# Attention block with layer norm and a quantised layer on one core: TensorE takes the score products two slots at a time, and SyncE issues all the loads of the row layout

## The chip, the cores and the metric

The kernel runs on one core of one Trainium2 chip. The metric is the device time of one execution in microseconds (us). The time of the kernel before is the median of three timed runs. One further execution was taken by the hardware profiler, and all rows below come from that one.

## What is computed

There are 16 batches of 256 tokens with 128 features, and 16 heads of width 8. In every batch the reference does this (cut to what matters):

```python
mod = (silu(c) @ wmod).reshape(16, 6, 1, -1)        # sa, ca, ga, sb, cb, gb; ga and gb kept away from 0
h = layernorm(x) * (1 + ca) + sa
qkv = h @ W_qkv + b_qkv                              # q, k, v: 16 heads of 8
energy = einsum('bqhe,bkhe->bqhk', q, k)
attn = softmax(energy, axis=-1) / sqrt(128)
o = einsum('bihv,bvhd->bihd', attn, v).reshape(16, 256, 128)
x = x + ga * (o @ W_out + b_out)
h = layernorm(x) * (1 + cb) + sb
x = x + gb * (fp6_blocks(h) @ fp6_blocks(weight).T + bias)   # blocks of 32, grid e2m3, one scale per block
```

## The kernel before

All five engines run one software pipeline over batches. The outer loop on each engine is `for b in STEPS`, with b from -4 to 17, and inside it are 16 **slots** s = 0 to 15, one per head of batch b. In slot s of step b TensorE computes two score products, each as two matmuls of 256 columns:

- `scores2(b, s, t)` (line 809) writes the transposed scores of head s of batch b, with the row maxima subtracted, into one of **two** PSUM banks `ps_p2`. ScalarE reads it with `exponentials` (line 551) and writes `probs`. The product of slot s waits for the exponential of slot s - 2.
- `scores1` (line 794) works `LEAD = 20` slots ahead: it writes the plain scores of a later head into one of **three** banks `ps_p1`. VectorE reads it with `maxima` (line 684) for the row maxima. The product of a slot waits for the maxima of the slot three before.

The two products use opposite halves of the 128 array rows (`q_rows` and `k_rows` at partitions 0 to 63 or 64 to 127), so their matmuls are written alternately: one of `scores1`, one of `scores2`, one of `scores1`, one of `scores2`.

Between the slots TensorE does all its **other** products, each behind a slot named in the code. Below they have short names: `tx` (transposes of the normalised x, line 835, slot 0), v3 (`values(b-1, 3)`, slot 1), `hd` (transposes of the quantised rows, line 890, slot 1), `pq` and `pk` (projections to q and k, line 851, slots 2 and 4), `to` (`transpose_o`, line 868, slot 3), `lin` (line 896, slot 3), `tn` (`transpose_norm`, line 876, slot 5), v0 (`values(b, 0)`, line 824, slot 6), `po` (`project_out`, line 882, slot 6), `pv` (`project_v`, line 845, slot 7), `tm` (`transpose_max`, line 858, slots 8 and 14), v1 (slot 10) and v2 (slot 13). `values(b, v)` is 16 matmuls at 32 columns of weights that need the exponentials of slots 4v to 4v + 3.

ScalarE runs its exponentials in the same 16 slots. Behind some it copies PSUM banks out: `save_hT` (line 524, slot 1), `oT`, `hdT` and `onT` (line 555, slots 1, 2, 5), `save_qk` (lines 531 and 532, slots 3 and 5), `save_v` (line 537, slot 7), `save_maxT` (line 543, slots 8 and 14). VectorE runs maxima in the same slots with the layer norms and residuals between them.

q and k are projected for pairs of batches. `tx`, `pq` and `pk` run in odd steps b = 1 to 11 only (in the start also at b = -3 and -2), and `stats1` and `aggregate1` on VectorE (slots 4 and 5) in even steps 0 to 10 only. GpSimd makes the low part of q and k (`low_part`), and SyncE stores high and low parts to `parts_dram` (`store_parts`, lines 358 and 363). Then `lay_out(eng, p, kind, r)` (line 330) reads them back into `q_rows` and `k_rows`, 512 KB for each of kind q, k and half r = 0, 1. Pair p is first read by `scores1` in slot 12 of the next even step. SyncE issues the two with r = 0. ScalarE issues the two with r = 1 in slots 11 and 12 of the odd step, and each waits for the store of its kind. SyncE also carries the row maxima of the next batch into `q_rows` (`place_max`, line 370, half 0 and half 1). `scores2` needs half 0 in slot 0 and half 1 in slot 8 of the next step.

The order on each engine is the order in which the code is written.

## Time and profile of the kernel before

| | |
|---|---|
| median of three timed runs | 344.18 us (343.35 to 344.89) |
| the profiled execution | 341.19 us |
| its span in the trace | 339.3 us |
| granted TensorE clock, mean of the span | 0.923 |
| TensorE, VectorE, ScalarE, GpSimd busy | 82%, 72%, 61%, 51% |
| one odd step (b = 9), sc14 to sc14 | 224.45 - 205.75 = 18.70 us |
| one even step (b = 10), sc14 to sc14 | 240.08 - 224.45 = 15.63 us |

In what follows sc9 means both score products of slot 9, exp9 and max9 the exponential and the maxima of slot 9. The busy time of TensorE counts matmuls of both halves of the array rows, and matmuls are pipelined, so its share alone doesn't say that TensorE is the bound. Which engine sets the pace is read in the timeline of a step: who waits for whom. The profiled execution is 3 us faster than the median of the timed runs.

### The profile page before, as it was taken

How to read it: one execution, taken by the hardware profiler on the slowest of the kernel's cores; microseconds unless marked ns; L12 is line 12 of the kernel's file. 1: busy time of each engine (PE TensorE's matmuls, PEld its weight loads, DVE VectorE, ACT ScalarE, POOL GpSimd, SP SyncE). 2: the span in 40 equal slices, each digit the busy share in tenths (PEclk: the TensorE clock that was granted, in tenths of full speed). 3: DMA queues.
4: the chain of work that ended last, by engine and by line, in shares of the span. 5: the costliest groups of instructions: out<-in, count | busy, mean ns of one | idle time of the engine just before them, and what ended most of it. 6: DMA issues, size and time to landing. Idle time of an engine off the chain costs nothing.

```text
span 339.3 us, 7143 instructions
## 1 busy us (share of the span) xinstructions
PE 279.7 (82%) x2506; PEld 171.2 (50%) x2506; DVE 243.4 (72%) x581; ACT 207.5 (61%) x404; POOL 174.5 (51%) x330
## 2 busy tenths in 40 slices
PE   0831886989999999999998899899989999999742
PEld 0310764545555555555655565556555656555421
DVE  6577775667897679767976797679768878872243
ACT  6262014577668667777677667776777776677510
POOL 5910122316665656566665657575757364645620
PEclk9975555899999999999999999999999999999985
DMA  4679189016911692169316931495149510100000
GB/s 150 199 269 226 35 288 236 9 36 251 251 50 34 265 244 59 35 256 209 103 33 238 214 114 36 192 223 150 36 175 237 152 37 18 35 20 17 2 15 15
DMA packets 23970, 43.81 MB, mean 129 GB/s; under 512 B 2144, under 2 KB 7408, under 8 KB 23936
## 3 DMA queue, kind: packets, MB, share of 16 engines
q1 hardware_dynamic: 20128, 36.03, 35.0%
q10 hardware_dynamic: 3808, 7.34, 9.0%
q8 instruction: 20, 0.33, 0.4%
q14 instruction: 14, 0.11, 0.1%
HBM read 23.93 MB, written 18.91 MB: 126 GB/s over the span
## 4 chain that ended last, share of the span: by engine, by line
PE 55%; ACT 12%; issue 10%; DVE 9%; DMA 9%; POOL 4%; SPq 1%; ACTq 0%; DVEq 0%; POOLq 0%
PE ps_o L824 16%; PE ps_p L794 15%; PE ps_p L809 7%; ACT probs L551 5%; PE ps_pre L851 4%; DVE neg_max L684 3%; DMA parts_dram<-qk_parts 3%; PE ps_post L882 3%; PE ps_pre L845 3%; DMA k_rows<-parts_dram 3%; ACT qk_full_sb L531 2%; ACT qk_parts L532 2%; DMA q_rows<-maxT 2%; PE ps_post L890 2%; PE ps_pre L858 2%
## 5 line engine op out<-in xcount | busy, mean ns | idle before, releaser
L684 DVE TENSOR_REDUCE neg_max<-ps_p 128x2 f32<-128x512 f32 x256 | 165.4, 683 | 49.0 <-PE ps_p L794 48.0
L551 ACT ACTIVATE probs<-ps_p 128x512 f32<-128x512 f32 x256 | 146.2, 596 | 77.5 <-PE ps_p L809 73.8
L809 PE MATMUL ps_p<-q_rows,k_rows 64*128 64x256 f32 x512 | 117.1, 327 | 13.9 <-ACT probs L551 9.7
L794 PE MATMUL ps_p<-k_rows,q_rows 62*128 62x256 f32 x512 | 119.9, 339 | 8.1 <-DMA k_rows<-parts_dram 8.1
L794 PEld LDWEIGHTS ps_p<-k_rows,q_rows 62*128 62x128 f32 x512 | 79.4, 198 | 48.0 <-DVE neg_max L684 22.5
L809 PEld LDWEIGHTS ps_p<-q_rows,k_rows 64*128 64x128 f32 x512 | 74.3, 189 | 24.6 <-ACT probs L551 18.2
L824 PE MATMUL ps_o<-probs,v_aug 128*32 128x256 f32 x1024 | 69.4, 389 | 0.9 <-ACT probs L551 0.9
L429 POOL CAST max_parts<-neg_max 128x16 fp32r<-128x16 f32 x32 | 6.3, 196 | 74.3 <-DVE neg_max L684 74.3
L824 PEld LDWEIGHTS ps_o<-probs,v_aug 128*32 128x32 f32 x1024 | 26.9, 110 | 21.0 <-ACT probs L551 1.4
L448 POOL TENSOR_TENSOR rstd<-ve,minus_half 128x2 f32<-128x2 f32 x16 | 11.3, 704 | 35.1 <-DVE ve L609 35.1
L319 POOL TENSOR_TENSOR qk_parts<-qk_full_sb,qk_parts 128x512 fp32r<-128x512 f32 x14 | 17.7, 1266 | 17.0 <-ACT qk_parts L532 17.0
L851 PE MATMUL ps_pre<-hT,wqkv_sb 128*128 128x512 f32 x28 | 17.5, 709 | 9.2 <-ACT hT L524 5.8
L704 DVE TENSOR_TENSOR x<-ps_post,x_res 128x256 f32<-128x256 f32 x16 | 6.7, 420 | 15.5 <-PE ps_post L882 15.5
L537 ACT ACTIVATE v_aug<-ps_pre 128x256 f32<-128x256 f32 x16 | 6.1, 383 | 16.2 <-PE ps_pre L845 16.0
L543 ACT ACTIVATE maxT<-ps_pre 16x256 fp32r<-16x256 f32 x32 | 11.4, 357 | 6.0 <-DMA parts_dram<-qk_parts 5.4
L441 POOL TENSOR_SCALAR xhat<-x_all,nm,rstd 128x128 f32<-128x128 f32 x32 | 14.4, 461 | 0.8
L296 POOL TENSOR_SCALAR xh<-x,nm,rstd 128x128 f32<-128x128 f32 x30 | 13.1, 448 | 1.6
L438 POOL TENSOR_TENSOR rstd<-ve,minus_half 128x4 f32<-128x4 f32 x8 | 8.2, 1019 | 11.0 <-DVE ve L609 10.9
L311 POOL TENSOR_TENSOR hq<-h,rs 128x256 fp8e4<-128x256 f32 x15 | 9.2, 616 | 8.8 <-DVE rs L730 8.8
L882 PE MATMUL ps_post<-wout_b,onT 128*128 128x128 f32 x64 | 11.4, 301 | 2.6 <-ACT onT L555 2.6
L882 PEld LDWEIGHTS ps_post<-wout_b,onT 128*128 128x128 f32 x64 | 8.3, 190 | 9.4 <-ACT onT L555 5.7
L896 PE MATMUL ps_post<-wf_b,hdT 128*128 128x128 f32 x64 | 11.3, 301 | 2.0 <-ACT hdT L555 1.9
(104 smaller groups left out, 354.4 us busy)
## 6 DMA issues: line engine op xcount, KB each, us to landing
parts_dram<-qk_parts SPq DMA_DIRECT2D x8, 1024.0 KB, 4.4
parts_dram<-qk_parts SPq DMA_DIRECT2D x16, 512.0 KB, 3.8
q_rows<-parts_dram SPq DMA_DIRECT2D x9, 512.0 KB, 5.1
k_rows<-parts_dram SPq DMA_DIRECT2D x9, 512.0 KB, 9.1
modb<-mod_rows_dram SPq DMA_DIRECT2D x16, 256.0 KB, 3.3
q_rows<-parts_dram ACTq DMA_DIRECT2D x7, 512.0 KB, 7.0
k_rows<-parts_dram ACTq DMA_DIRECT2D x7, 512.0 KB, 10.5
out_dram<-out_sb SPq DMA_DIRECT2D x16, 128.0 KB, 1.7
```

The lines of the kernel that those rows point to most:

```text
L296: ins = eng.tensor_scalar(xh2[:, n, :], x1[:, n, :], nm2[:, n:n + 1], rstd2[:, n:n + 1], ALU.add, ALU.mult)
L319: eng.tensor_tensor(qk_parts[:, p % 2, kind, 1, :], qk_full_sb[:, kind, :], qk_parts[:, p % 2, kind, 0, :].bitcast(F32), ALU.subtract).the ...
L441: ins = pool.tensor_scalar(xhat[:, n, :], x_all[:, 2 * p + n // 2, n % 2, :], nm1[:, n:n + 1], rstd1[:, n:n + 1], ALU.add, ALU.mult)
L448: pool.tensor_tensor(rstd2[:, :], ve2[:, :], minus_half[:, 0:QT], ALU.pow).then_inc(rstd2_ready, 1)
L543: act.activation(maxT[:, half, :], ps_pre[0:16, 0:T], ACT.Copy).then_inc(maxT_saved, 1)
L551: act.activation(probs[:, v % 2, u % 4, :], ps_p2[:, u % 2, :], ACT.Exp).then_inc(exp_done, 1)
L684: dve.tensor_reduce(neg_max[:, half, :, r, j], ps_p1[:, (16 * b + s) % P1_BANKS, :].rearrange("p (q k) -> p q k", q=QT), AX_X, ALU.max, ne ...
L794: ins = pe.matmul(ps_p1[:, (16 * b + s) % P1_BANKS, t * T:(t + 1) * T], q_rows[64 * r:64 * r + ROWS1, slot, i, e, t * P:(t + 1) * P], k_ro ...
L809: ins = pe.matmul(ps_p2[:, u % 2, t * T:(t + 1) * T], k_rows[64 * r:64 * r + ROWS2, slot, i, e, t * P:(t + 1) * P], q_rows[64 * r:64 * r + ...
L824: ins = pe.matmul(ps_o[32 * j:32 * j + 32, half * T:(half + 1) * T], at[:, 2 * D * r:2 * D * r + 32], probs[:, v % 2, j, t * T:(t + 1) * T ...
L851: pe.matmul(bank[:, :], wqkv_sb[:, kind * E:(kind + 1) * E], hT[:, p % 2, :], start=True, stop=True).then_inc(full, 1)
L882: ins = pe.matmul(ps_post[:, t * P:(t + 1) * P], onT[:, t * P:(t + 1) * P], wout_b[:, b % 2, :], start=True, stop=True)
```

## The change

Three things are edited.

- TensorE: the loop over slots does the score products of slots s and s + 1 together where s is even, and nothing of them where s is odd. The other products stay in the order they had. Those that stood behind slot s (even) now stand behind the score products of s + 1.
- ScalarE no longer issues layout loads.
- SyncE issues all four layout loads of a pair one after the other, between the two halves of `place_max`, where it issued two.

`project_v` stays at slot 7.

```diff
                 if p is not None:
-                    lay_out(sp, p, 0, 0)
-                    lay_out(sp, p, 1, 0)
+                    for kind in range(2):
+                        for r in range(2):
+                            lay_out(sp, p, kind, r)
                 if has(b + 1):
                     place_max(b + 1, 1)
...
-                    if s in (11, 12) and low_pair(b) is not None:
-                        lay_out(act, low_pair(b), s - 11, 1)
...
                 for s in range(16):
-                    if has1(b, s):
-                        before_scores1(*at1(b, s))
-                        scores1(*at1(b, s), 0)
-                    if has(b):
-                        before_scores2(b, s)
-                        scores2(b, s, 0)
-                    if has1(b, s):
-                        scores1(*at1(b, s), 1)
-                    if has(b):
-                        scores2(b, s, 1)
+                    for u in (s, s + 1) if s % 2 == 0 else ():
+                        if has1(b, u):
+                            before_scores1(*at1(b, u))
+                            scores1(*at1(b, u), 0)
+                        if has(b):
+                            before_scores2(b, u)
+                            scores2(b, u, 0)
+                        if has1(b, u):
+                            scores1(*at1(b, u), 1)
+                        if has(b):
+                            scores2(b, u, 1)
```

**Between v1 and v2.** TensorE in an odd step, before, from the second half of slot 11 to v2. `ps_p1` rows are `scores1`, `ps_p2` rows are `scores2`, four rows are one slot:

```order
L794 MATMUL ps_p1<-k_rows,q_rows 128x256
L809 MATMUL ps_p2<-q_rows,k_rows 128x256
L794 MATMUL ps_p1<-k_rows,q_rows 128x256
L809 MATMUL ps_p2<-q_rows,k_rows 128x256
L794 MATMUL ps_p1<-k_rows,q_rows 128x256
L809 MATMUL ps_p2<-q_rows,k_rows 128x256
L794 MATMUL ps_p1<-k_rows,q_rows 128x256
L809 MATMUL ps_p2<-q_rows,k_rows 128x256
L794 MATMUL ps_p1<-k_rows,q_rows 128x256
L809 MATMUL ps_p2<-q_rows,k_rows 128x256
L824 MATMUL ps_o<-probs,v_aug 32x256 x8
```

Three slots (11, 12, 13) stood between v1 and v2. The same place after the change, from v1 to v2:

```order
L823 MATMUL ps_o<-probs,v_aug 32x256 x8
L793 MATMUL ps_p1<-k_rows,q_rows 128x256
L808 MATMUL ps_p2<-q_rows,k_rows 128x256
L793 MATMUL ps_p1<-k_rows,q_rows 128x256
L808 MATMUL ps_p2<-q_rows,k_rows 128x256
L793 MATMUL ps_p1<-k_rows,q_rows 128x256
L808 MATMUL ps_p2<-q_rows,k_rows 128x256
L793 MATMUL ps_p1<-k_rows,q_rows 128x256
L808 MATMUL ps_p2<-q_rows,k_rows 128x256
L823 MATMUL ps_o<-probs,v_aug 32x256 x8
```

Now two slots (12, 13) stand there, and slot 11 has moved ahead of v1.

**The other half of that trade.** TensorE in the same step, before, from tm of slot 8 to v1:

```order
L858 MATMUL ps_pre<-ident_r,max_parts 16x128 x2
L794 MATMUL ps_p1<-k_rows,q_rows 128x256
L809 MATMUL ps_p2<-q_rows,k_rows 128x256
L794 MATMUL ps_p1<-k_rows,q_rows 128x256
L809 MATMUL ps_p2<-q_rows,k_rows 128x256
L794 MATMUL ps_p1<-k_rows,q_rows 128x256
L809 MATMUL ps_p2<-q_rows,k_rows 128x256
L794 MATMUL ps_p1<-k_rows,q_rows 128x256
L809 MATMUL ps_p2<-q_rows,k_rows 128x256
L824 MATMUL ps_o<-probs,v_aug 32x256 x8
```

The row count between tm and v1 is the same after the change, but the slots in it are 10 and 11, where they were 9 and 10: slot 9 now stands ahead of tm, so its exponential still comes behind the `save_maxT` that waits for tm.

**The layout loads.** ScalarE, before, in an odd step from the copy of `maxT` in slot 8 to that in slot 14:

```order
L543 ACTIVATE maxT<-ps_pre 16x256
L551 ACTIVATE probs<-ps_p2 128x512 x3
L330 DMA q_rows<-parts_dram 32x8x512
L551 ACTIVATE probs<-ps_p2 128x512
L330 DMA k_rows<-parts_dram 32x8x512
L551 ACTIVATE probs<-ps_p2 128x512 x2
L543 ACTIVATE maxT<-ps_pre 16x256
```

SyncE after the change, from the stores of an odd step to the load of the next batch's rows:

```order
L358 DMA parts_dram<-qk_parts 256x1x1024
L363 DMA parts_dram<-qk_parts 128x2x512 x2
L370 DMA q_rows<-maxT 2x4x256 x2
L330 DMA q_rows<-parts_dram 32x8x512 x2
L330 DMA k_rows<-parts_dram 32x8x512 x2
L370 DMA q_rows<-maxT 2x4x256 x2
L378 DMA modb<-mod_rows_dram 128x512
```

The two DMA rows of ScalarE are gone, and each L330 row of SyncE stands for two loads where it was one. The second `place_max` (the lower L370 row) now stands behind four loads.

## Rows read from the trace of the kernel before

**Rows 1.** The profile's page: busy time of each engine

```profile
PE 279.7 (82%) x2506; PEld 171.2 (50%) x2506; DVE 243.4 (72%) x581; ACT 207.5 (61%) x404; POOL 174.5 (51%) x330
```

**Rows 2.** Waits of the whole span: total us, times, longest us

```profile
ACT probs L551 <- PE ps_p L809: 73.8, 88, 3.3
DVE neg_max L684 <- PE ps_p L794: 48.0, 59, 4.0
```

**Rows 3.** Timeline, TensorE, odd step from v1: start us, us, engine, line, operation

```profile
220.80 1.07 PE L824 MATMUL ps_o<-probs,v_aug 128*32 128x256 f32 x16
...
223.02 0.38 PE L809 MATMUL ps_p<-q_rows,k_rows 64*128 64x256 f32 x1 [0.35 <-ACT probs L551]
...
223.45 1.07 PE L824 MATMUL ps_o<-probs,v_aug 128*32 128x256 f32 x16
224.45 0.38 PE L794 MATMUL ps_p<-k_rows,q_rows 62*128 62x256 f32 x1
...
226.40 0.38 PE L809 MATMUL ps_p<-q_rows,k_rows 64*128 64x256 f32 x1 [0.23 <-ACT probs L551]
```

**Rows 4.** Timeline, TensorE, start and first half of that odd step

```profile
205.75 0.38 PE L794 MATMUL ps_p<-k_rows,q_rows 62*128 62x256 f32 x1
...
207.41 0.66 PE L835 MATMUL ps_pre<-ident,xhat 128*128 128x128 f32 x4
207.99 0.38 PE L794 MATMUL ps_p<-k_rows,q_rows 62*128 62x256 f32 x1
...
213.75 1.10 PE L851 MATMUL ps_pre<-hT,wqkv_sb 128*128 128x512 f32 x2 [0.50 <-ACT qk_parts L532]
...
217.43 0.71 PE L882 MATMUL ps_post<-wout_b,onT 128*128 128x128 f32 x4 [0.35 <-ACT onT L555]
...
219.15 0.38 PE L794 MATMUL ps_p<-k_rows,q_rows 62*128 62x256 f32 x1
```

**Rows 5.** Timeline, TensorE, slots 2 and 3 of an even step, adjacent already

```profile
193.94 0.38 PE L794 MATMUL ps_p<-k_rows,q_rows 62*128 62x256 f32 x1
...
194.60 0.66 PE L868 MATMUL ps_o<-ident,oT 128*128 128x128 f32 x4
```

**Rows 6.** Timeline, ScalarE, slots 8 to 11 of the odd step

```profile
219.72 0.60 ACT L551 ACTIVATE probs<-ps_p 128x512 f32<-128x512 f32 x1
220.21 0.36 ACT L543 ACTIVATE maxT<-ps_pre 16x256 fp32r<-16x256 f32 x1
220.57 1.09 ACT L551 ACTIVATE probs<-ps_p 128x512 f32<-128x512 f32 x2
```

**Rows 7.** Timeline, TensorE and VectorE, slots 10 to 14 of an even step

```profile
236.42 1.07 PE L824 MATMUL ps_o<-probs,v_aug 128*32 128x256 f32 x16
...
240.08 0.38 PE L794 MATMUL ps_p<-k_rows,q_rows 62*128 62x256 f32 x1
...
236.63 3.22 DVE L684 TENSOR_REDUCE neg_max<-ps_p 128x2 f32<-128x512 f32 x5
```

**Rows 8.** Timeline, ScalarE, odd step b = 7 with a late store

```profile
190.28 1.08 ACT L551 ACTIVATE probs<-ps_p 128x512 f32<-128x512 f32 x2 [1.79 <-PE ps_p L809]
```

**Rows 9.** The chain that ended last: v1 of steps b = 6 and 8 (us, us)

```profile
167.21 1.00 PE ps_o L824 x16
...
202.17 1.00 PE ps_o L824 x16
```

**Rows 10.** b = 5: issue of the last k load, sc8 of b = 6, us to landing

```profile
153.64 0.32 ACTq L330 DMA_DIRECT2D k_rows<-parts_dram  x1
...
165.49 0.38 PE L794 MATMUL ps_p<-k_rows,q_rows 62*128 62x256 f32 x1
...
k_rows<-parts_dram ACTq DMA_DIRECT2D x1, 512.0 KB, 11.9
```

**Rows 11.** The chain that ended last, start of the pipeline: start us, us

```profile
46.78 6.74 DMA q_rows<-maxT
```

**Rows 12.** DMA issues from 44 to 62 us: count, KB, us to landing

```profile
parts_dram<-qk_parts SPq DMA_DIRECT2D x2, 512.0 KB, 5.3
```

## The prediction, made before the changed kernel ran

> **What bounds the kernel now.** I read the page first [rows 1]: TensorE is busy for 82% of the span and no other engine for more than 72%. Next the waits [rows 2]: ScalarE waits 73.8 us for score products and VectorE 48.0 us. So in the middle of the kernel TensorE's order sets the pace, and the wait for an exponential decides at a few places. Then I read the timeline of one odd step, from sc14 at 205.75 to sc14 at 224.45, 18.70 us, and of the even step behind it, to 240.08, 15.63 us [rows 3, 4, 7]. There are six odd steps with projections (b = 1 to 11) and nine that look like the even one (b = 0, the other even ones to 14, and 13).
>
> **The costs of slots.** Two adjacent slots take 194.60 - 193.94 = 0.66 us up to the next product of another kind [rows 5]. A lone slot takes 223.45 - 223.02 = 0.43 us (sc13 up to v2) [rows 3]. So joining two slots saves 0.22 us, and a slot added to a group costs 0.22 us. An exponential takes about 0.60 us and its successor starts 0.55 us behind it (two in 1.09); a copy of maxT takes its place for 0.36 us [rows 6]. From the start of a product to its exponential it is 219.72 - 219.15 = 0.57 us [rows 4, 6], and for the second slot of a joined pair some 0.23 us more.
>
> **The odd step, by its parts.**
>
> 1. *sc14 to sc1.* This stretch hangs on ScalarE: exp14, the copy of maxT, exp15, then sc1, since `ps_p2` has two banks. In the even step without `tx` it is 226.40 - 224.45 = 1.95 us [rows 3]. The pair doesn't shorten it: exp15 still stands behind a copy that waits for tm. Before an odd step it is 207.99 - 205.75 = 2.24 us, because `tx` stood between sc0 and sc1 and filled the wait [rows 4]. Now sc1 starts at 1.98 and `tx` comes after it, so the filler is lost: -0.26 here, +0.58 (207.99 - 207.41) in the next part.
>
> 2. *sc1 to v1.* Before: 220.80 - 207.99 = 12.81 us [rows 3, 4]. Out of it go three joins (2 and 3, 4 and 5, 6 and 7), 3 x 0.22 = 0.66. Two waits go too, the 0.50 of `pk` for the copy of q and the 0.35 of `po` for the copy of onT [rows 4], with 0.06 each for the step from semaphore to matmul, and 0.2 in front of tm, which waited for the copy of v: 1.2 together. They go because a slot now stands between each of these products and what it needs: `pk` behind sc5 and not sc4, `po` behind sc7. Added are `tx`, 0.58, and slot 11, 0.22. Without a new wait v1 would stand at 12.81 - 0.66 - 1.2 + 0.58 + 0.22 = 11.7 us. But a new wait comes in. sc8 starts at about 10.1, and exp8 at 10.7. The copy of maxT needs tm, which now stands behind sc9, and starts at 11.2. Exp9 ends at 12.1, and only then may sc11 start, at 12.2. So v1 starts at 12.6, and 0.9 of the gain is lost again.
>
> 3. *v1 to sc14.* Before: 224.45 - 220.80 = 3.65 us [rows 3]. Behind v1 slots 11, 12 and 13 are adjacent, but with two banks the third waits for exp11, which cannot start before sc11 is out: sc11 starts with the end of v1, which takes 1.00 [rows 9], at 221.80, and sc13 only at 223.02, 1.22 later [rows 3]. With two slots between v1 and v2, both banks are free when v1 ends, and the stretch is 1.00 + 0.66 + 1.00 = 2.66 us, a gain of 1.0.
>
> Sum: 1.98 + 12.6 + 2.66 = 17.23 against 18.70, a gain of 1.47 us. Bounds: 0.5, if the two waits of part 2 don't go, and 2.4, if the new wait for exp9 doesn't come. I take 1.47, since each of its steps has its row. Six times: 8.8 us.
>
> **The even step.** sc14 to sc1 stays at 1.98. From sc1 to v1 it was 236.42 - 226.40 = 10.02 us [rows 3, 7]. Slots 0 to 5 stood adjacent in pairs already, so nothing is won there. Slots 6 and 7 are joined, but sc7 now waits for exp5 and v0 starts 0.5 later; the same wait for exp9 puts v1 at sc8 + 2.04 + 0.43, about 10.9, so +0.9. From v1 to sc14: 240.08 - 236.42 = 3.66 before, 2.66 after [rows 7], -1.0. Sum -0.13; nine times -1.2 us. What hides the 0.9 is the stretch behind it. VectorE could take that cover away: max9 to max13 come there in a row from 236.63 to 239.85, 0.64 each [rows 7]. sc13 needs max10, which ends at 237.9 now and at about 238.2 in the new order (`po` and with it the residual come 0.3 later), and sc13 wants it at 238.5. That is 0.3 us of room.
>
> **The loads.** ScalarE's own issues run beside an exponential (0.3 us each) and cost nothing to speak of. The waits in front of them do cost: in the odd step b = 7 the store of k was late, the load waited for it, and the exponential behind the load started 1.79 us after the one ahead had ended, so the score products that wait for its bank came late too [rows 8]. The same happens at b = 3. From v1 of b = 6 to v1 of b = 8 it is 34.96 us [rows 9], against 18.70 + 15.63 = 34.33 for the two steps read above: 0.6 us that can go. I count 1.0 for both places. On SyncE what is queued behind the two moved loads is `place_max` half 1, then `modb` and the output store. `place_max` half 1 has a date: sc8 of the next even step. For b = 5 the last load of k was issued at 153.64 and landed 11.9 us later, at 165.5, and sc8 stands at 165.49 [rows 10]. That is the tightest of the six. So if `place_max` now lands behind all four loads, b = 6 waits some tenths and the others hardly. I set this against the 1.0 us and take 0 for both; ends -1.0 and +3.
>
> The Trainium skill speaks against this edit: "DMA: Bandwidth & Descriptors", section "Queues, rings and completion order", says that each DMA engine takes turns between the queues of SyncE and ScalarE, packet by packet, and works one queue in order. By that rule `place_max` half 1 had to let two loads pass and now has to let four pass, which is the rival B below; the trace of before gives no landing for it that would show this.
>
> **The start.** The first `scores2` waits for `place_max` half 0, issued at 46.78 and landed 6.74 us later [rows 11]. ScalarE's first load of q goes out beside it. The stores ahead on SyncE's queue landed 5.3 us after their issue in the two microseconds before, so by some 50.2 [rows 12]. With that load now behind on SyncE's queue, `place_max` may land up to 3.3 us sooner, or no sooner, since the bytes in flight otherwise stay. Of 3.3 at most half could be kept, because `place_max` half 1 would then be late for sc8. I take 0.5, nearer to no gain, as the bytes stay. In the last 32 us there are no pairs that wait; I take 0 for them (-0.5 to +0.5).
>
> **The sum.** 8.8 + 1.2 + 0.5 = 10.5 us. The profiled execution took 341.19 us, so the same one would take 330.7 us. The median of the timed runs is 344.18, so the forecast for the median is 333.7 us, 3.1% less.
>
> **The rivals.**
>
> A. *The bunched exponentials and maxima are not caught up, slower.* Place: even step, slots 9 to 13. If sc12 and sc13 find max9 or max10 late, the 0.9 lost at v1 stays and the 1.0 behind it isn't won: +0.9 nine times, and in the odd steps a gain of only 0.47 six times: +8.1 - 2.8 = +5.3, 349.5 us. It decides from the point at which max10 ends over 1.3 us later than I put it (0.3 of room and the 1.0). For it: VectorE runs five maxima without a gap up to 239.85 [rows 7]. Against: over the whole span it waits 48.0 us for products [rows 2].
>
> B. *`place_max` half 1 comes late for sc8.* The last landing would have to be 1.5 us later than now in each of six even steps, 9 us lost: 342.7 us. For it: room of 0 us at b = 6 [rows 10]. Against: the room elsewhere, and the loads as a whole move no more bytes.
>
> C. *Only the joins count.* The waits of part 2 go, but others of the same size come (`lin` for the copy of hdT, `pk` all the same). Then 0.9 per odd step and nothing elsewhere: 5.4 us, 338.8 us. For it: ScalarE has four copies in slots 1 to 3. Against: none of them ends later than 0.3 us ahead of its reader in my walk.
>
> D. *The pair is none in practice.* sc of s + 1 waits for exp of s - 1 each time, so the pairs fall apart, and the products behind them are only shifted: gain and loss cancel, 344 us.
>
> **How the numbers follow.** The forecast 0.50 (330 to 337), C 0.18, B 0.12, D 0.08, A 0.09, and 0.03 for less than 330. Range 330 to 343: it takes in C, B, and the best ends of start and loads (10.5 + 1 + 2 = 13.5); A, D and the tail below are left out, 0.2. Half a percent, 1.7 us, is about what a measurement of this kernel can tell from no change. Faster by over that: forecast, C, the tail and half of B, 0.77. Within: D and the other half of B, 0.14. Slower: 0.09.
>
> **What would show it.** In the new trace: odd step (sc14 to sc14) near 17.2 us and even near 15.5; v1 to sc14 2.7 us in both; the wait in front of sc11 on exp9 about 0.9 us in every step, a wait that the old trace doesn't have; `pk` and `po` without a wait; sc1 ahead of `tx` and about 0.3 us sooner behind sc14. Against it would speak: sc13 still waiting between v1 and v2 (A), sc8 of even steps waiting for a DMA `q_rows<-maxT` (B), `pk` or `lin` waiting for ScalarE (C). The forecast is wrong if v1 to sc14 stays above 3.3 us.

## The result and the profile of the changed kernel

The changed kernel takes **333.04 us** (median, 332.22 to 333.23) against 344.49 us for the kernel before, run beside it: ratio 0.967, 95% interval 0.964 to 0.970. The forecast was 333.7. The profiled execution took 332.22 us (span 330.4), against 341.19 us (span 339.3) for the one on which the sum was made: 9.0 us of gain where the sum said 10.5. Some executions of some kernels below had a lower granted clock than the others and took over 1.5% longer: the medians are taken over all executions, the ratios without these, and where too few were left (e1, e8, e11) no ratio is given and I use the trace, for the length of the steps.

The page's busy times first, the line that answers to [rows 1], then the waits, the first two of which answer to [rows 2]; the last one has no counterpart in the middle of the kernel before.

```profile
PE 274.4 (83%) x2506; PEld 171.4 (52%) x2506; DVE 243.9 (74%) x581; ACT 207.3 (63%) x404; POOL 174.8 (53%) x330
```

```profile
ACT probs L552 <- PE ps_p L808: 46.4, 68, 2.5
DVE neg_max L683 <- PE ps_p L793: 36.6, 48, 4.0
...
ACT v_aug L538 <- PE ps_pre L844: 32.6, 16, 16.2
...
PE ps_p L808 <- DMA q_rows<-maxT: 4.6, 6, 2.1
```

ScalarE waits 27 us less for score products and VectorE 11 us less. But ScalarE's waiting has partly moved and not gone: for the projection to v (`v_aug`) it now waits 32.6 us in 16 waits, where it was 16.0 us in 2. The remaining 11 us are near the 9 us by which the kernel is shorter. TensorE now waits six times for `place_max`, once at sc0 of step 0 and five times at sc8.

The odd step b = 9 again, TensorE's timeline from sc14 to sc14, as in [rows 3, 4]:

```profile
200.55 0.38 PE L793 MATMUL ps_p<-k_rows,q_rows 62*128 62x256 f32 x1
...
202.51 0.38 PE L808 MATMUL ps_p<-q_rows,k_rows 64*128 64x256 f32 x1 [0.24 <-ACT probs L552]
...
208.17 1.12 PE L850 MATMUL ps_pre<-hT,wqkv_sb 128*128 128x512 f32 x2
...
211.11 0.71 PE L881 MATMUL ps_post<-wout_b,onT 128*128 128x128 f32 x4
...
213.45 0.38 PE L793 MATMUL ps_p<-k_rows,q_rows 62*128 62x256 f32 x1 [0.29 <-DVE neg_max L683]
...
214.15 0.38 PE L808 MATMUL ps_p<-q_rows,k_rows 64*128 64x256 f32 x1
...
214.58 1.07 PE L823 MATMUL ps_o<-probs,v_aug 128*32 128x256 f32 x16
...
216.25 1.07 PE L823 MATMUL ps_o<-probs,v_aug 128*32 128x256 f32 x16
217.25 0.38 PE L793 MATMUL ps_p<-k_rows,q_rows 62*128 62x256 f32 x1
...
218.30 0.29 PE L857 MATMUL ps_pre<-ident_r,max_parts 128*16 128x128 f32 x2 [0.32 <-POOL max_parts L432]
```

`pk` (208.17) and `po` (211.11) start without a wait; before, they waited 0.50 and 0.35 us. v1 to v2 is 216.25 - 214.58 = 1.67 us, before 2.65: sc13's wait is gone, and one slot fewer stands there. The whole step is 217.25 - 200.55 = 16.70 us, before 18.70. The last row is new: tm waits for GpSimd's split of the maxima.

sc8 of two even steps, with SyncE's issue of the `place_max` half 1 that the one at 163.02 needs (the first in step b = 0, the other in b = 6):

```profile
61.48 0.35 PE L808 MATMUL ps_p<-q_rows,k_rows 64*128 64x256 f32 x1 [2.06 <-DMA q_rows<-maxT]
...
163.02 0.35 PE L808 MATMUL ps_p<-q_rows,k_rows 64*128 64x256 f32 x1 [0.86 <-DMA q_rows<-maxT]
...
153.11 1.28 SPq L370 DMA_DIRECT2D q_rows<-maxT  x2
```

The same wait stands at b = 2, 4 and 10 with 0.47, 0.53 and 0.38 us. At b = 8 and 12 the trace names no wait, but the second product of sc8 starts 0.4 us behind the first, where in a kernel with `place_max` in time (e6 below) both start together. The issue ended at 154.39, and sc8 went out 8.6 us later.

The time of the whole kernel can be read off the starts of v1. Three stretches, from the profiled executions, us:

| stretch | before | after | difference |
|---|---|---|---|
| start to v1 of b = 2 | 98.10 | 98.91 | +0.8 |
| v1 of b = 2 to v1 of b = 12 (five odd, five even steps) | 172.64 | 164.44 | -8.2 |
| v1 of b = 12 to the end | 68.6 | 67.0 | -1.5 |

The middle gained what the sum gave it (five times 1.47 + 0.13 is 8.0). The start lost where it should have gained, and the windows show how. Each row has the stretch, its length, TensorE's busy time and matmuls, the granted clock, the DMA share and GB/s; the wait ended at 61.48.

```profile
60.00:62.00 2.00, 0.52 (x7) 1.00 0.58 131
62.00:64.00 2.00, 2.00 (x13) 0.55 0.00 0
64.00:66.00 2.00, 2.00 (x18) 0.50 0.02 8
66.00:68.00 2.00, 2.00 (x20) 0.50 0.00 0
68.00:70.00 2.00, 2.00 (x23) 0.74 0.00 0
```

The clock had been at its full level, 2.4 GHz, since 58.8. Behind the idle stretch of 2 us it fell to its half level, 1.2 GHz, and stayed there to about 69 us, with TensorE busy all the time.

### The profile page after: what moved, and what is told of

Its sections match the earlier page's. It is cut to its first block, busy times and chain, and to the rows that moved or that the text cites. A ratio compares the mean times of both kernels' runs of the same rounds, so it can differ in the third digit from the quotient of the medians.

```text
span 330.4 us, 7143 instructions
## 1 busy us (share of the span) xinstructions
PE 274.4 (83%) x2506; PEld 171.4 (52%) x2506; DVE 243.9 (74%) x581; ACT 207.3 (63%) x404; POOL 174.8 (53%) x330
## 4 chain that ended last, share of the span: by engine, by line
PE 35%; DMA 23%; DVE 12%; POOL 11%; issue 8%; ACT 7%; SPq 3%; POOLq 0%; ACTq 0%; DVEq 0%
DMA q_rows<-maxT 13%; PE ps_o L823 11%; PE ps_p L793 7%; DMA parts_dram<-qk_parts 7%; PE ps_p L808 6%; DVE neg_max L683 5%; PE ps_pre L850 3%; ACT probs L552 3%; DMA k_rows<-parts_dram 3%; POOL qk_parts L319 2%; POOL xh L296 2%; PE ps_post L881 2%; POOL rstd L449 2%; ACT maxT L544 2%; POOL xm L300 2%
## 5 line engine op out<-in xcount | busy, mean ns | idle before, releaser
L683 DVE TENSOR_REDUCE neg_max<-ps_p 128x2 f32<-128x512 f32 x256 | 163.3, 682 | 37.0 <-PE ps_p L793 36.6
L552 ACT ACTIVATE probs<-ps_p 128x512 f32<-128x512 f32 x256 | 143.4, 594 | 50.5 <-PE ps_p L808 46.4
L793 PE MATMUL ps_p<-k_rows,q_rows 62*128 62x256 f32 x512 | 115.9, 337 | 11.7 <-DMA k_rows<-parts_dram 8.6
L808 PE MATMUL ps_p<-q_rows,k_rows 64*128 64x256 f32 x512 | 107.4, 319 | 11.6 <-ACT probs L552 6.7
L808 PEld LDWEIGHTS ps_p<-q_rows,k_rows 64*128 64x128 f32 x512 | 72.8, 191 | 23.6 <-ACT probs L552 14.8
L823 PE MATMUL ps_o<-probs,v_aug 128*32 128x256 f32 x1024 | 71.1, 397 | 0.9 <-ACT probs L552 0.9
L538 ACT ACTIVATE v_aug<-ps_pre 128x256 f32<-128x256 f32 x16 | 6.1, 384 | 32.6 <-PE ps_pre L844 32.6
L319 POOL TENSOR_TENSOR qk_parts<-qk_full_sb,qk_parts 128x512 fp32r<-128x512 f32 x14 | 17.7, 1269 | 12.6 <-ACT qk_parts L533 12.6
L439 POOL TENSOR_TENSOR rstd<-ve,minus_half 128x4 f32<-128x4 f32 x8 | 8.2, 1019 | 11.0 <-DVE ve L608 10.9
L532 ACT ACTIVATE qk_full_sb<-ps_pre,bqkv_col 128x512 f32<-128x512 f32 x14 | 9.6, 687 | 5.6 <-PE ps_pre L850 5.5
L556 ACT ACTIVATE oT<-ps_o 128x512 f32<-128x512 f32 x16 | 9.6, 598 | 5.2 <-PE ps_o L823 5.1
L889 PE MATMUL ps_post<-ident,hd 128*128 128x128 f32 x32 | 7.2, 310 | 6.6 <-DVE hd L314 6.6
```

The costliest lines, as they stand in the source:

```text
L319: eng.tensor_tensor(qk_parts[:, p % 2, kind, 1, :], qk_full_sb[:, kind, :], qk_parts[:, p % 2, kind, 0, :].bitcast(F32), ALU.subtract).the ...
L552: act.activation(probs[:, v % 2, u % 4, :], ps_p2[:, u % 2, :], ACT.Exp).then_inc(exp_done, 1)
L683: dve.tensor_reduce(neg_max[:, half, :, r, j], ps_p1[:, (16 * b + s) % P1_BANKS, :].rearrange("p (q k) -> p q k", q=QT), AX_X, ALU.max, ne ...
L793: ins = pe.matmul(ps_p1[:, (16 * b + s) % P1_BANKS, t * T:(t + 1) * T], q_rows[64 * r:64 * r + ROWS1, slot, i, e, t * P:(t + 1) * P], k_ro ...
L808: ins = pe.matmul(ps_p2[:, u % 2, t * T:(t + 1) * T], k_rows[64 * r:64 * r + ROWS2, slot, i, e, t * P:(t + 1) * P], q_rows[64 * r:64 * r + ...
L823: ins = pe.matmul(ps_o[32 * j:32 * j + 32, half * T:(half + 1) * T], at[:, 2 * D * r:2 * D * r + 32], probs[:, v % 2, j, t * T:(t + 1) * T ...
```

## Experiments

Line numbers are those of each kernel. A "pair of steps" is an odd and an even step, v1 of b = 2 to v1 of b = 12 divided by five. All results in one table; "start" is v1 of b = 2 in the profiled execution.

| kernel | median us | ratio, 95% interval | start | pair of steps |
|---|---|---|---|---|
| before | 343.2 to 344.5 | 1 | 98.10 | 34.53 |
| after | 333.04 | 0.967 (0.964 to 0.970) | 98.91 | 32.89 |
| loads alone (e2) | 342.96 | 1.000 (0.996 to 1.004) | 99.82 | 34.54 |
| pairs alone (e1) | 345.76 | none | 102.41 | 34.79 |
| the same kernel again (e1b) | 343.83 | 0.993 (0.989 to 0.998) | 99.88 | 34.82 |
| pairs, ScalarE's loads later (e8) | 336.39 | none | 99.08 | 33.14 |
| after, half 1 on ScalarE (e3) | 333.46 | 0.965 (0.957 to 0.974) | 95.60 | 33.72 |
| after, copies late (e4) | 328.97 | 0.958 (0.950 to 0.965) | 95.94 | 32.44 |
| e3 and e4 (e5) | 332.01 | 0.968 (0.963 to 0.972) | 98.08 | 32.90 |
| after, half 1 before k (e6) | 325.47 | 0.949 (0.945 to 0.952) | 93.74 | 32.56 |
| e6 and e4 (e9) | 322.41 | 0.939 (0.933 to 0.945) | 93.62 | 32.11 |
| e6, pairs in slots 0 to 7 alone (e10) | 331.56 | 0.965 (0.958 to 0.971) | 95.25 | 33.00 |
| e6, pairs in slots 8 to 15 alone (e11) | 340.35 | none | 99.10 | 33.92 |
| e6 without pairs (e12) | 340.32 | 0.989 (0.986 to 0.993) | 96.22 | 34.33 |

### Either part of the change alone

The pairs with the loads where they were (e1; e1b is the same kernel with more executions), and the moved loads with TensorE's old order (e2). The edit of e1 to the changed kernel:

```
-                    for kind in range(2):
-                        for r in range(2):
-                            lay_out(sp, p, kind, r)
+                    lay_out(sp, p, 0, 0)
+                    lay_out(sp, p, 1, 0)
...
+                    if s in (11, 12) and low_pair(b) is not None:
+                        lay_out(act, low_pair(b), s - 11, 1)
```

> The pairs alone: TensorE's new order, with the four layout loads shared between SyncE and ScalarE as in the kernel before. Theory (the pairs bring the whole gain, the moved loads cost something): place_max half 1 no longer waits behind four loads, so the waits of the changed kernel for q_rows<-maxT at sc8 (2.06, 0.47, 0.53, 0.86 and 0.38 us) go, and with the 2.06 the stretch at half clock behind it; the late stores at some odd steps cost ScalarE 0.5 us each again. 328 to 331 us against 333.0 of the changed kernel. Rival (moving the loads was worth about 1 us by itself): 334 us.

> The kernel with the pairs and with two of the four layout loads on ScalarE again, the same as in the first look, timed in more rounds, since that look gave 339 to 347 us and no ratio. Theory: with the pairs, slots 11 and 12 come sooner against the store of k, so ScalarE waits for that store in front of its load in every odd step (124.31 [1.57], 192.55 [0.59], 261.00 [0.53] in the first trace) and the exponentials behind it come late. Then the time is really 339 to 346 us, and the ratio lies between 0.985 and 1.005. Rival: the first look was a poor draw and the pairs alone bring what they bring with the loads moved, 333 to 336 us, ratio below 0.98.

> The loads alone: TensorE's order of before, all four layout loads on SyncE. Theory: place_max half 0 lands 3 us sooner at the start, but half 1 comes late for sc8 of b = 0 by 1 to 2 us and by some tenths in the later even steps, and ScalarE's waits for late stores go (1.0 us): 343 to 348 us against 344.5 of before, not faster. Rival (the moved loads carry a part of the gain): 340 us or less.

The loads alone bring nothing, as I expected. **The pairs alone bring next to nothing either**: by the ratio 0.2% to 1.1%, where I had expected nearly the whole gain, and the twelve executions of e1b spread from 338.3 to 351.3 us. Together the two parts bring 3.3%. So they need each other, which the prediction did not see. The trace of e1b shows two new waits in most pairs of steps. Step b = 5, ScalarE with its two loads, then TensorE at sc0 of b = 6, then SyncE's `place_max` half 0:

```profile
153.37 0.31 ACTq L330 DMA_DIRECT2D q_rows<-parts_dram  x1
...
155.66 0.36 ACTq L330 DMA_DIRECT2D k_rows<-parts_dram  x1
156.07 1.09 ACT L551 ACTIVATE probs<-ps_p 128x512 f32<-128x512 f32 x2 [0.69 <-DMA parts_dram<-qk_parts]
...
158.81 0.35 PE L809 MATMUL ps_p<-q_rows,k_rows 64*128 64x256 f32 x1 [1.05 <-DMA q_rows<-maxT]
...
152.27 1.71 SPq L370 DMA_DIRECT2D q_rows<-maxT  x2
```

First, the pairs bring slots 11 and 12 on ScalarE closer to the store of k, so the load in ScalarE's queue stands waiting for the store and the exponentials wait behind it, 0.7 to 2.1 us in five odd steps (before, so large a wait stood at two places [rows 8]). Second, ScalarE's load of q goes out at 153.37, while `place_max` half 0 is still being issued; sc0 gets its rows only at 158.81, 4.8 us after the issue ended. In the changed kernel no other queue is in the way and sc0 never waits for half 0 in the middle of the kernel.

Behind these waits the granted clock falls too, in five places, to its half level for 3 to 7 us, with TensorE busy throughout. The longest follows a wait of 1.63 us for an exponential at 121.83 (windows as above):

```profile
124.00:126.00 2.00, 2.00 (x19) 0.50 1.03 280
126.00:128.00 2.00, 2.00 (x15) 0.50 0.98 284
```

Four of the five lie in the five pairs of steps. From v3 to the next v0, where no wait reaches 0.25 us, those steps take 6.7 to 7.5 us, while the changed kernel always takes 5.6. That makes 5.4 us; the five pairs of steps of e1b are 9.6 us longer than those of the changed kernel. So the waits cost about as much again through the clock behind them.

To tell whether it is the place of ScalarE's loads or their being there at all, e8 keeps the two queues and issues the loads behind exp13 and exp15:

```
-                    if s in (11, 12) and low_pair(b) is not None:
-                        lay_out(act, low_pair(b), s - 11, 1)
+                    if s in (13, 15) and low_pair(b) is not None:
+                        lay_out(act, low_pair(b), (s - 13) // 2, 1)
```

> Pairs, and ScalarE's two layout loads stay on its queue but stand behind exp13 and exp15 instead of behind exp11 and exp12. The store of k is then over when ScalarE reaches its load. Theory (ScalarE's wait for the store is what the pairs alone lose): no wait for parts_dram on ScalarE, 333 to 336 us. Rival (two queues of layout loads at once make place_max half 1 late, wherever ScalarE's loads stand): waits of 0.7 to 1.5 us for q_rows<-maxT in front of sc8 stay in every even step and the time stays above 339 us.

(The waits of e1 that this text puts at sc8 stand at sc0: they are for half 0.) ScalarE no longer waits for a store in its trace, and the pair of steps falls from 34.82 to 33.14 us, the median to 336.4. The loss of the pairs alone was thus the wait in ScalarE's queue and the load of q beside half 0, with the falls of the clock behind them (e8 takes both waits away at once and doesn't tell how they share the loss); two queues as such cost little in this trace. Its four executions lie between 333.8 and 341.2 us and the profiled one is at the lower end. What its trace has above the changed kernel stands in one step, where a short wait is followed by a fall of the clock:

```profile
195.77 0.35 PE L809 MATMUL ps_p<-q_rows,k_rows 64*128 64x256 f32 x1 [0.43 <-DMA q_rows<-maxT]
198.09 1.94 PE L824 MATMUL ps_o<-probs,v_aug 128*32 128x256 f32 x16
201.11 1.20 PE L824 MATMUL ps_o<-probs,v_aug 128*32 128x256 f32 x16
```

```profile
198.00:200.00 2.00, 2.00 (x21) 0.51 0.02 8
```

v1 to v2 takes 3.02 us there instead of 1.67.

### Why `place_max` half 1 is late

Theory one: its place behind the loads in SyncE's queue. Theory two: the loads' bytes in flight, whichever queue it stands in. e3 gives half 1 a queue of its own (ScalarE issues it behind exp15), all loads still on SyncE:

```
-                if has(b + 1):
-                    place_max(b + 1, 1)
...
+                    if s == 15 and has(b + 1):
+                        place_max(act, b + 1, 1)
```

> The changed kernel with place_max half 1 issued by ScalarE behind exp15, so on a queue that has no layout loads. Theory (it is late because it stands in SyncE's queue behind four loads): no wait at sc8 for q_rows<-maxT in any step; the idle 2 us of TensorE in step 0 go, and its clock rises to the full level some 7 us sooner; step 0 takes 16 us and not 21, and the later even steps gain 2.2 us in all: 325 to 328 us. Rival (it is late because the DMA engines are full with the loads, whichever queue it is in): the waits stay, 332 to 334 us.

The wait of step 0 goes and with it the stretch at half clock (start 95.60). But the time stays at 333.46 us. Half 1 is issued at 151.93 to 153.21 on its own queue, and sc8 of b = 6 starts at 161.68 behind a wait of 0.71 us, 8.5 us later; behind all four loads in one queue it was 8.6 us. In step 0 it gains somewhat more: half 1 reaches its reader 8.4 us after its issue, in the changed kernel 9.2, and sc8 goes out at 61.05 where it was 61.48. The wait of 2.06 us is gone there mainly because TensorE comes to sc8 1.5 us later (60.56, in the changed kernel 59.04). So the place in the queue is not it, or for less than 1 us of it. The DMA engines have no time to spare: in the windows of the changed kernel around these loads their share is over 1.0 (columns as above).

```profile
152.00:156.00 4.00, 3.28 (x38) 1.00 1.08 226
156.00:160.00 4.00, 3.68 (x38) 1.00 1.05 215
```

In e3 the clock also fell in the steps b = 4 and 8 (v1 to v2 2.99 and 2.97 us), which took the gain of the start back.

e6 then leaves the queue alone and issues half 1 ahead of the two loads of k, whose first reader is the plain product beside slot 12 of the next step:

```
-                    for kind in range(2):
-                        for r in range(2):
-                            lay_out(sp, p, kind, r)
+                    for r in range(2):
+                        lay_out(sp, p, 0, r)
                 if has(b + 1):
                     place_max(b + 1, 1)
+                if p is not None:
+                    for r in range(2):
+                        lay_out(sp, p, 1, r)
```

> The changed kernel with place_max half 1 issued ahead of the two loads of k on SyncE's queue instead of behind them. Theory (the bytes of the loads ahead make place_max half 1 late): the waits of 0.4 to 0.9 us in front of sc8 of even steps and the 2.06 us in step 0 go, and the time is 329 to 331 us. The loads of k are needed 16 slots later, in front of the plain score product with slot 12; issued at about 121.5 instead of 119.4 in the step of 105 to 121 us they land at about 131, which is just when it starts. Rival (that date is missed): the wait only moves to slot 12, and the time is 333 us or more.

**325.47 us**, better than either expectation. Half 1 itself goes out no sooner: its issue begins 4.46 us behind v1 of b = 5 in both kernels (153.11 - 148.65, here 147.80 - 143.34). What changed is that the loads of k, 1 MB, are issued behind it and not ahead. No sc8 waits for `place_max` any more, and nothing waits for the loads of k, which now land in 7.4 us (9.6 in the changed kernel). Every odd step is 17.05 us and every even one 15.52, to 0.02. Of the 6.6 us by which the profiled span is shorter than that of the changed kernel, 5.2 stand in the start: 2.2 at v1 of b = 0, which is the wait, 2.2 in the step behind it, where the changed kernel ran at half clock, and 0.8 in the next. Only 1.6 stand in the middle. Its profiled execution had the full clock from the first microsecond, but that is not the reason: two of its four executions had a mean clock of 0.987 and spans of 323.8 us, the two others 0.93 and 323.4 and 322.2.

e12 makes the same swap in the old order, without pairs:

```
-                    for u in (s, s + 1) if s % 2 == 0 else ():
+                    for u in (s,):
```

> No pairs at all: TensorE's order of the kernel before, all loads on SyncE, place_max half 1 ahead of the loads of k. Theory: in the old order place_max was in time for sc8 except in step 0 (61.96 [1.38]) and in one step at the end, so the swap brings only the start, some 3 to 4 us: a pair of steps stays at 34.3 us and the time is 338 to 341 us. Rival (the swap is worth as much in either order): 335 us or less.

340.32 us: by the medians the swap is worth 2.6 us over e2. In the profiled spans it is 3.6: 3.6 in the start (99.82 to 96.22) and 1.0 in the steps, which the end gives back. In the new order it was 7.6 us by the medians and 6.6 by the spans. So 3 to 5 us of it exist only because the pairs made sc8 come sooner. Put the other way: with half 1 in time the pairs are worth 340.32 - 325.47 = 14.9 us (14.9 by the spans too), with half 1 behind the loads 342.96 - 333.04 = 9.9 (11.9 by the spans). These kernels were not all timed side by side, and the kernel before moved by 1.3 us between the occasions, so a us or two of such differences is not certain.

### Which pairs bring the gain

e10 and e11 are e6 with pairs in one half of the slots alone. The edit is that of e10; e11 has `s >= 8` in place of `s < 8`:

```
-                    for u in (s, s + 1) if s % 2 == 0 else ():
+                    for u in ((s, s + 1) if s % 2 == 0 else ()) if s < 8 else (s,):
```

> The loads as in the kernel with place_max half 1 ahead of the loads of k; slots 0 to 7 in pairs, slots 8 to 15 one by one as before. By the steps of the prediction this half brings the gain of the odd step (joins, the waits of pk and po): 12.81 - 0.66 - 1.2 + 0.58 = 11.53 from sc1 to v1, with no wait for exp9 and no slot 11 ahead of v1, and 3.65 as before behind it. A pair of steps then takes 34.33 - 1.5 = 32.8 us against 32.57 with all pairs, and the time is 326 to 329 us. Rival: the gain comes from the second half (v1 to v2 in 1.67 instead of 2.65 us), and this kernel stands at 333 us or more.

> The same loads; slots 0 to 7 one by one as before, slots 8 to 15 in pairs. By the steps of the prediction the 1.0 us won between v1 and v2 is what the wait for exp9 (0.9) and slot 11 ahead of v1 (0.22) cost, so a pair of steps stays at 34.2 to 34.6 us and the time is 334 to 339 us. Rival: this half brings the gain, 327 us or less.

v1 of b = 9 and b = 10, e10, then e11 and e6 with v1 of b = 8 ahead (timelines of TensorE):

```profile
211.50 1.07 PE L825 MATMUL ps_o<-probs,v_aug 128*32 128x256 f32 x16
...
227.24 1.07 PE L825 MATMUL ps_o<-probs,v_aug 128*32 128x256 f32 x16
```

```profile
200.85 1.07 PE L825 MATMUL ps_o<-probs,v_aug 128*32 128x256 f32 x16
...
219.39 1.07 PE L825 MATMUL ps_o<-probs,v_aug 128*32 128x256 f32 x16
...
234.77 1.07 PE L825 MATMUL ps_o<-probs,v_aug 128*32 128x256 f32 x16
```

```profile
191.42 1.07 PE L825 MATMUL ps_o<-probs,v_aug 128*32 128x256 f32 x16
...
208.47 1.07 PE L825 MATMUL ps_o<-probs,v_aug 128*32 128x256 f32 x16
...
223.99 1.07 PE L825 MATMUL ps_o<-probs,v_aug 128*32 128x256 f32 x16
```

| order, half 1 in time | odd step | even step | both |
|---|---|---|---|
| no pairs (e12) | 18.70 | 15.64 | 34.33 |
| slots 0 to 7 (e10) | 17.26 | 15.74 | 33.00 |
| slots 8 to 15 (e11) | 18.54 | 15.38 | 33.92 |
| all (e6) | 17.05 | 15.52 | 32.57 |
| predicted change, all | -1.47 | -0.13 | -1.60 |
| measured change, all | -1.65 | -0.12 | -1.76 |

The halves add up: -1.33 and -0.41 make -1.74. The first half brings the gain, in the odd step, as the prediction's parts have it. The trace of e11 still has both of its waits, `pk` and `po`, with the very lengths of [rows 4]:

```profile
211.62 1.10 PE L852 MATMUL ps_pre<-hT,wqkv_sb 128*128 128x512 f32 x2 [0.50 <-ACT qk_parts L535]
...
215.30 0.71 PE L883 MATMUL ps_post<-wout_b,onT 128*128 128x128 f32 x4 [0.35 <-ACT onT L558]
```

The second half brings 0.4 us for two steps where I had expected a loss or nothing. The time of e10, 331.56 us, is above my 326 to 329: five pairs of steps explain 2.2 of its 6.1 us against e6; 1.5 more stand in the start and 2.1 behind v1 of b = 12, where I had put no effect of pairs at all. e11 I had expected at 334 to 339 us. One of its four executions took 334.3 and three took 339.6 to 341.6 us, so its time settles little and the steps are what I use.

### What comes next in the path

e4 moves the two copies of maxT on ScalarE behind exp9 and exp15, so that no exponential for which TensorE waits stands behind a copy; e5 adds to it half 1 on ScalarE behind exp0 of the next step:

```
-                    if s == 8 and has(b + 1):
+                    if s == 9 and has(b + 1):
                         save_maxT(b + 1, 0)
...
-                    if s == 14 and has(b + 1):
+                    if s == 15 and has(b + 1):
                         save_maxT(b + 1, 1)
```

> The changed kernel with ScalarE's two copies of maxT one slot later (behind exp9 and exp15), so that exp9 and exp15 don't stand behind a copy that waits for tm. Theory (in the pairs' order the copies hold up exp9 and exp15, and with them sc11 and sc1): sc14 to sc1 0.3 us shorter and sc8 to v1 0.1 us shorter in odd and 0.3 us in even steps, so some 5 us less: 328 us. Rival A (VectorE's maxima or GpSimd's chain to hd are as late as the exponentials): less than 1.5 us gained, 332 us.

> The changed kernel with the copies of maxT one slot later (behind exp9 and exp15, 328.97 us by itself) and place_max half 1 issued by ScalarE behind exp0 of the next step instead of by SyncE behind the loads (333.46 us by itself, without the 2 us wait of step 0). If the two gains add: the wait of step 0 goes and the clock is full from 64 us on, some 2 to 4 us more than the late copies alone, 325 to 327 us. Rival (place_max half 1 is late in the even steps whichever queue issues it, and what the start gains is lost at sc8): 328 to 330 us.

> place_max half 1 ahead of the loads of k (325.47 us by itself) and the two copies of maxT on ScalarE one slot later (328.97 by itself, 4 us under the changed kernel, with waits for q_rows<-maxT still in it). Theory: the two edits take away different waits (a DMA at sc8; exp9 and exp15 behind a copy), so a pair of steps falls from 32.57 to about 31.8 us, seven times 0.8 is 5 to 6 us, and the time is 319 to 322 us. Rival: with the copy late, place_max half 1 goes out half a microsecond to a microsecond later and the loads of k behind it too, so that the plain score product with slot 12 waits for them or sc8 waits again; then 324 to 326 us.

e4 brings 4 us, where I had expected 5. But only 2.2 of them stand in the five pairs of steps; 3.0 stand in the start, where sc8 still waits 2.19 us and the stretch at half clock behind it lasts 4 us and not 7.

e5 is no faster than e4 and probably slower (332.01 against 328.97 us; the intervals of the ratios overlap at 0.963 to 0.965), above both of its expectations. As its rival says, sc8 waits for `place_max` again, seven times, up to 1.07 us. But half 1 goes out no later than in e4, 4.6 us behind v1 of b = 5 in both. What is new is a pause of ScalarE in every step, 0.73 to 0.90 us, behind the issue of the two small DMAs:

```profile
152.06 1.28 ACTq L336 DMA_DIRECT2D q_rows<-maxT  x2
153.38 0.60 ACT L550 ACTIVATE probs<-ps_p 128x512 f32<-128x512 f32 x1 [0.73 <-issue]
```

Its odd steps take 16.75 us where those of e4 take 16.35. No run tells the pause and the waits apart.

e9, with half 1 ahead of k and late copies, is the fastest kernel of the study, **322.41 us, ratio 0.939**. It is 3 us below e6; I had expected 319 to 322 us, with a pair of steps of 31.8 us (32.11 measured). The exponentials no longer hold sc1, and TensorE waits for GpSimd instead, twice in every step, once for the split of the maxima and once for the quantised rows (TensorE's timeline from v1 of b = 9 into the even step behind it):

```profile
206.69 1.07 PE L825 MATMUL ps_o<-probs,v_aug 128*32 128x256 f32 x16
208.35 1.07 PE L825 MATMUL ps_o<-probs,v_aug 128*32 128x256 f32 x16
...
210.52 0.29 PE L859 MATMUL ps_pre<-ident_r,max_parts 128*16 128x128 f32 x2 [0.43 <-POOL max_parts L434]
211.49 1.07 PE L825 MATMUL ps_o<-probs,v_aug 128*32 128x256 f32 x16
213.00 0.44 PE L891 MATMUL ps_post<-ident,hd 128*128 128x128 f32 x2 [0.44 <-POOL hd L314]
```

## Why the prediction was right, and where it was not

**The odd and even step: right in size.** With `place_max` out of the way (e6 against e12) the odd step fell by 1.65 us and the even one by 0.12, against 1.47 and 0.13. Two of the parts were off and cancelled. Part 1, sc14 to sc1, was to be 1.98 us and is 2.30 in e6, ahead of odd and of even steps. What I had not priced is the wait of tm for GpSimd's split (rows from the start of b = 10):

```profile
212.20 0.29 PE L859 MATMUL ps_pre<-ident_r,max_parts 128*16 128x128 f32 x2 [0.33 <-POOL max_parts L434]
...
213.44 0.38 PE L810 MATMUL ps_p<-q_rows,k_rows 64*128 64x256 f32 x1 [0.40 <-ACT probs L554]
```

tm comes sooner than the maxima that it transposes, its copy and exp15 follow it, and sc1 waits for exp15. Part 2, sc1 to v1, was to be 12.6 us in the odd step and is 208.47 - 196.38 = 12.09: up to sc8 0.4 less than in my walk, and from sc8 to v1 2.4 us (214.58 - 212.20 in the changed kernel) instead of 2.5. Part 3, v1 to sc14, was to be 2.66 us and is 2.67. In the even step the same two parts cancel: 2.30 for 1.98, and 10.55 for 10.9.

**The wait for exp9: its length right, its cause half right.** ScalarE in the changed kernel, behind sc8 at 212.20:

```profile
213.27 0.36 ACT L544 ACTIVATE maxT<-ps_pre 16x256 fp32r<-16x256 f32 x1
213.53 1.75 ACT L552 ACTIVATE probs<-ps_p 128x512 f32<-128x512 f32 x3
```

The copy starts 1.07 us behind sc8 (1.1 in the sum), exp9 follows it, and sc11's product for ScalarE goes out at 214.15, 1.95 behind sc8 (2.1). But there is no wait of 0.9 us in front of sc11, as I had named for a sign. A part stands at sc10, which waits 0.29 us for VectorE's maxima (213.45 above). And e4, where exp9 no longer stands behind the copy, needs 4.37 us from v0 to v1 of b = 9 against 4.47. So VectorE, which the sum left out here, holds this stretch nearly as long as ScalarE.

**The middle: partly luck.** The 8.2 us gained there come from three numbers: by the steps of e6 and e12 the pairs gain 5 x 1.76 = 8.8; the late stores of the kernel before had cost 1.0 (5 x (34.53 - 34.33), before against e12), as I had put it; and `place_max` half 1 costs 1.6. I had 8.0 for the first and nothing for the other two together. The forecast of the median, 333.7 for 333.04, is closer than the sum was: on the profiled executions the sum is 1.5 us too high, and the median of the kernel before, from which the forecast counts, lies 3 us above its profiled execution, that of the changed kernel 0.8.

**The split between odd and even step in the changed kernel: wrong.** There the odd step is 16.70 us and the even one 16.19 (v1 of b = 8, 9, 10: 197.88, 214.58, 230.77), so -2.0 and +0.57 where I had -1.47 and -0.13. The failed step is "sc8 of the next even step", for which I took 0 and "some tenths" at b = 6 alone: half 1 held up sc8 by 0.4 to 2.1 us in all seven even steps up to b = 12, in five of them as a wait that the trace names. The wait makes the even step longer, and GpSimd and ScalarE catch up in it, so that the odd step's tm no longer waits (sc14 to sc1 1.96 us, and 2.30 in e6). A part of the delay is thus given back: 32.89 against 32.57 us for two steps.

**The loads: the number right, the reason not.** Taken alone they are worth nothing (e2), as in the sum. But I costed them in the old order, and in the new one they take the ratio from 0.993 to 0.967. The pairs shorten the room between the store of k and ScalarE's load, and between half 0 and sc0. I had looked for queues behind the moved loads and not for what the pairs would do to the loads if they stayed.

**The rivals.** B happened in kind: sc8 waits for `q_rows<-maxT`. Its price of 1.5 us in six steps was too high for the middle of the kernel (1.6 us in all) and left out where it was dear, in the start. A did not come: sc13 does not wait and v1 to sc14 is 2.67 us. C and D did not come either: `pk`, `po` and `lin` have no new wait over 0.2 us, and the pairs stay pairs. New waits of 0.3 us, of the kind that C speaks of, stand at tm and sc10 instead.

**The start: wrong in sign.** `place_max` half 0 landed 3 us sooner, at the upper end that I gave (the first product of the pipeline starts at 50.55, before at 53.56). I had said that half 1 would then be late for sc8, and it was, by 2.06 us. What failed is the step from there to a gain of 0.5: the idle 2 us were followed by 7 us at half the clock, and 0.8 us were lost instead. With e6 the start gains 4.4 us over before.

**The end: mis-sized.** I took 0 for the last 32 us, at most 0.5. Of the 1.5 us gained behind v1 of b = 12, 0.9 stand behind v1 of b = 15 (22.5 to 21.6 us).

**The queues.** I had set the rule of the Trainium skill ("DMA: Bandwidth & Descriptors", section "Queues, rings and completion order") against the moved loads: a DMA engine takes turns between queues and works one queue in order. In e1b `place_max` half 0 is late when a load of the other queue starts beside it, which fits taking turns. But a queue of its own (e3) brought half 1 hardly sooner, 8.5 us against 8.6 in b = 6 and 8.4 against 9.2 in step 0, where turns alone would let a small transfer pass the loads. What helped was to have fewer bytes issued ahead of it (e6). No run shows how much of the loads one turn takes, so why a queue of its own didn't help stays open.

## What to carry to other kernels

When an order is tightened, look up every small transfer that has a date in it: here two DMAs of 8 KB behind 2 MB of loads cost a fifth to a third of what the new order could give (11.9 or 9.9 for 14.9 us), and moving them ahead of the loads that were not yet needed cost nothing. Cost a move of DMAs in the new order, not in the old: the same move was worth nothing before and about 3% after. And where TensorE waits 2 us in one place, read the granted clock of the 10 us behind it before putting the price at 2 us.

## What was not expected of the hardware

- A wait of 2.06 us was followed by a stretch of 7 us at half clock, and in e1b waits of 0.9 to 1.6 us by stretches of 3 to 7 us; in e8 and e3 waits of 0.3 to 0.45 us were followed, 2 to 3 us later, by a stretch of 2 to 3 us at half clock, which cost 1.3 us each time. In e9, waits of 0.4 us twice in every step left the clock at its full level, and so did waits of 0.5 to 0.9 us in the changed kernel. What tells these apart stays open.
- In e6 the clock in the first 64 us made no difference to the time: in most executions it is at half level from about 20 us on, in some at full level throughout, and e6 took 322.2 to 323.4 us (spans) with the one and 323.8 with the other. TensorE waits there for DMAs, among others 4.12 us for the first `place_max` in the kernel before.
- Two small DMAs issued on a queue with nothing else in it took 8.1 and 8.5 us to their reader (e3, b = 4 and 6) while 2 MB of loads were in flight on another queue, the same as behind them in their own queue (8.0 and 8.6).
- Issuing two small DMAs took ScalarE 1.28 us and kept its next exponential back by 0.73 to 0.90 us (e5), though a single load issued there, 0.31 us, ran beside an exponential.
